# The gate of a Mamba block computed on GpSimd, behind its additions, instead of on VectorE

## The reference

```
x = x + 0.5 * ffn(layernorm(x))          # 8 experts, top 2, 128 -> 512 -> 128, silu
x = x + mixer(layernorm(x))
x = x + 0.5 * ffn(layernorm(x))

mixer(x):   out1 = mamba(rmsnorm(x));  x1 = x + out1
            out2 = memory(mamba(rmsnorm(x1)));  return x1 + out2

mamba(u):   xm, res = split(u @ in_w + in_b)          # 256 channels each
            xm = silu(causal_conv(xm));  delta, B, C = projections of xm
            h[t] = h[t-1] * exp(delta*A) + delta*xm*B     # 16 states for each channel
            y = sum over states of h*C
            y = (y + xm * D_ssm) * silu(res)              # the gate: what is moved
            return y @ out_w + out_b
```

## Time and profile before

| | |
|---|---|
| median of the runs | 2010.15 us (2008.85 to 2011.12) |
| profiled execution | span 2008.6 us, from its first to its last instruction; no other time of it is given |
| PE | 1699.4 us busy (85%) |
| DVE | 1722.4 us (86%) |
| ACT | 1144.8 us (57%) |
| POOL | 748.6 us (37%) |
| mean granted TensorE clock | 0.865 |
| DVE: scans L912 | 256 of 2523 ns |
| DVE: gate, L930, L933, L936 | 32 x 682, 64 x 481, 32 x 692 ns |
| POOL: additions L1101 | 192 of 2866 and 32 of 2846 ns |

### The profile page before, as it was taken

The page is one execution under the profiler, slowest core; times in us unless marked ns, Lnnn a source line. Parts: engine busy times, 40 slices in busy tenths (PEclk is TensorE's granted clock), DMA queues, the critical chain, the costliest instruction groups (busy, mean ns, idle before and its releaser), DMA issues. The chain is left out here.

```text
span 2008.6 us, 26762 instructions
## 1 busy us (share of the span) xinstructions
PE 1699.4 (85%) x8800; PEld 1325.2 (66%) x8800; DVE 1722.4 (86%) x2419; ACT 1144.8 (57%) x2206; POOL 748.6 (37%) x366
## 2 busy tenths in 40 slices
PE   5779667889989898989899898998989899659778
PEld 4657535767767677767677676776767677436667
DVE  4269998999989998998989899898989899999931
ACT  3266554655756665656666566655756558436622
POOL 0005353444424244444324344243434444443310
PEclk9889767988989798998998799897989789668869
DMA  5000000000000000000000000000000000000000
GB/s 157 1 6 1 1 0 1 6 0 1 2 12 1 1 1 7 6 1 1 1 12 2 1 1 7 6 1 1 1 6 1 0 1 1 5 1 1 1 6 6
DMA packets 11432, 13.40 MB, mean 7 GB/s; under 512 B 400, under 2 KB 8592, under 8 KB 11152
## 3 DMA queue, kind: packets, MB, share of 16 engines
q1 hardware_dynamic: 11280, 11.51, 1.9%
HBM read 9.41 MB, written 2.10 MB: 6 GB/s over the span
## 5 line engine op out<-in xcount | busy, mean ns | idle before, releaser
L1101 POOL TENSOR_TENSOR acc<-acc,G 128x1024 f32<-128x1024 f32 x192 | 550.3, 2866 | 500.8 <-DVE G L922 495.1
L912 DVE TENSOR_TENSOR_SCAN hs<-dA,dbu 128x1024 f32<-128x1024 f32 x256 | 641.3, 2523 | 3.0 <-ACT dA L625 2.1
L568 ACT ACTIVATE raw<-b_h 128x512 f32<-128x512 f32 x512 | 305.4, 599 | 437.0 <-PE b_h L328 423.4
L625 ACT ACTIVATE dA<-delta,A 128x255 f32<-128x255 f32 x1024 | 423.0, 495 | 32.0 <-DVE hs L912 16.0
L922 DVE TENSOR_TENSOR G<-hs,b_r 128x1024 f32<-128x1024 f32 x256 | 310.0, 1211 | 29.3 <-PE b_r L407 21.3
L407 PE MATMUL b_r<-bcr,selr 64*128 64x256 f32 x1024 | 247.0, 346 | 89.6 <-DVE G L922 37.8
L902 DVE TENSOR_TENSOR dbu<-du,b_r 128x1024 f32<-128x1024 f32 x256 | 308.2, 1209 | 9.8 <-PE b_r L407 9.2
L326 PE MATMUL b_h<-xh,w1h 128*128 128x512 f32 x512 | 253.9, 496 | 73.3 <-DVE xa L838 26.4
L407 PEld LDWEIGHTS b_r<-bcr,selr 64*128 64x128 f32 x1024 | 162.2, 207 | 195.3 <-issue 89.2
L335 PE MATMUL b_h<-w2s,raw 128*128 128x128 f32 x2048 | 273.0, 286 | 0.0
L335 PEld LDWEIGHTS b_h<-w2s,raw 128*128 128x128 f32 x2048 | 251.3, 198 | 14.3 <-issue 4.5
(11 more groups left out here) (143 smaller groups left out, 1718.2 us busy)
## 6 DMA issues: line engine op xcount, KB each, us to landing
xin<-x_dram SPq DMA_DIRECT2D x8, 256.0 KB, 2.8
raw<-w_dram SPq DMA_DIRECT2D x1, 2048.0 KB, 11.5
out_dram<-ob SPq DMA_DIRECT2D x8, 256.0 KB, 2.3
prm<-pack_dram SPq DMA_DIRECT2D x1, 1124.5 KB, 5.2
dA<-early_dram SPq DMA_DIRECT2D x1, 512.0 KB, 11.8
hs<-sel_dram SPq DMA_DIRECT2D x2, 256.0 KB, 13.2
G<-sel_dram SPq DMA_DIRECT2D x2, 256.0 KB, 7.7
dbu<-early_dram SPq DMA_DIRECT2D x1, 384.0 KB, 11.9
```

What stands on the lines that cost most here:

```text
L568: do(hT[e % 2][:, c, :], H[i % 2][:, :], ACT.Silu).then_inc(f_hact, 1)
L625: last = do(dA[j % 4][:, d, k, 1:], delta[b][:, k, 1:], ACT.Exp, scale=A[:, k, s:s + 1])
L912: V.tensor_tensor_scan(flat(hs[j % 2]), flat(dA[j % 4]), flat(dbu[j % 2]), 0.0, ALU.mult, ALU.add)\
L1101: Q.tensor_tensor(acc[b][:, :, :, :], (G[0] if j == 1 else acc[b])[:, :, :, :], G[j % NG][:, :, :, :], ALU.add).then_inc(q_gs, 1)
```

## The change

The gate leaves VectorE's four lists and stands first in GpSimd's four lists, right behind a7 of the slot before and ahead of a1. GpSimd has no use for the combined multiply-add there: it multiplies xm by D_ssm into the first half of acc (two instructions of 128x256), adds that to yg, and multiplies by sres. That is five instructions and three drains where there were four and two. The waits are the same. TensorE's `memory_2` has one wait more, for the xb of the sequence before, which VectorE's order had implied so far.

```diff
     "vector": (
-        "gate flow b0 flog ftop b1 s0 s1 ...
+        "flow b0 flog ftop b1 s0 s1 ...
-        "f3 fstats gate b0 b1 s0 xsum s1 un ...
+        "f3 fstats b0 b1 s0 xsum s1 un ...
-        "flow b0 flog gate s0 b1 g0 xsum ...
+        "flow b0 flog s0 b1 g0 xsum ...
-        "f2 b0 b1 f3 s0 gate g0 b2 s1 s2 ...
+        "f2 b0 b1 f3 s0 g0 b2 s1 s2 ...
     "gpsimd": (
-        "a1 a2 a3 a4 a5 a6 a7",
-        "rms rs froot a1 a2 a3 a4 a5 a6 a7",
-        "rms a1 a2 rs lnx rmsx a3 a4 a5 a6 a7",
-        "a1 a2 a3 a4 froot a5 a6 a7"),
+        "gate a1 a2 a3 a4 a5 a6 a7",
+        "gate rms rs froot a1 a2 a3 a4 a5 a6 a7",
+        "gate rms a1 a2 rs lnx rmsx a3 a4 a5 a6 a7",
+        "gate a1 a2 a3 a4 froot a5 a6 a7"),
...
             def memory_2(g, b):
                 pe.wait_ge(g_oT, 2 * g + b + 1)
+                wait(pe, g_xb, 2 * g + b)
...
-            def gate_y(g, i):
-                q, b = 4 * g + i, i % 2
-                dve.wait_ge(q_gs, (q + 1) * (NP - 1))
-                dve.wait_ge(q_res, 2 * q + 2)
-                wait(dve, q_omm, q)
-                V.tensor_tensor(yg[:, :, :], acc[b][:, 0, :, :], acc[b][:, 1, :, :], ALU.add)
-                dve.drain()
-                for k in range(HALVES):
-                    V.scalar_tensor_tensor(out=yg[:, k, :], in0=xm[b][:, k, :], scalar=par("D_ssm")[:, k:k + 1],
-                                           in1=yg[:, k, :], op0=ALU.mult, op1=ALU.add)
-                dve.drain()
-                V.tensor_tensor(yg[:, :, :], yg[:, :, :], sres[b][:, :, :], ALU.mult).then_inc(q_yg, 1)
...
+            def gate_y(g, i):
+
+                q, b = 4 * g + i, i % 2
+                pool.wait_ge(q_gs, (q + 1) * (NP - 1))
+                pool.wait_ge(q_res, 2 * q + 2)
+                wait(pool, q_omm, q)
+                Q.tensor_tensor(yg[:, :, :], acc[b][:, 0, :, :], acc[b][:, 1, :, :], ALU.add)
+                pool.drain()
+                for k in range(HALVES):
+                    Q.tensor_scalar(acc[b][:, 0, k, :], xm[b][:, k, :], par("D_ssm")[:, k:k + 1], 0.0,
+                                    ALU.mult, ALU.add)
+                pool.drain()
+                Q.tensor_tensor(yg[:, :, :], yg[:, :, :], acc[b][:, 0, :, :], ALU.add)
+                pool.drain()
+                Q.tensor_tensor(yg[:, :, :], yg[:, :, :], sres[b][:, :, :], ALU.mult).then_inc(q_yg, 1)
```

More of the change, by code:

```diff
@@ L988, in slot @@
                                 square_norm(nxt, 0, ln, range(TILES))
[L989 to L992, removed]
+                    elif name in ("xsum", "mask", "xb"):
+                        if tail:
                             {"xsum": first_sum, "mask": masked, "xb": mixer_sum}[name](tail[0], tail[1] % 2)
@@ L1033, in finish @@
             def finish():
-                gate_y(GROUPS - 1, 3)
                 masked(GROUPS - 1, 1)
@@ L1114, in slot @@
                         pair_sum(g, i, num)
+                    elif name == "gate":
+                        if tail:
+                            gate_y(*tail)
                     elif name == "rms":
@@ L1135, in finish @@
             def finish():
+                gate_y(GROUPS - 1, 3)
                 ffn_root(second(GROUPS - 1))
```

## The result

The changed kernel takes 2041.26 us (median of 4 runs, 2038.94 to 2043.05), the kernel before 2009.50 us on the same chip (4 runs, 2008.69 to 2011.12): ratio 1.0159, 95% interval 1.0144 to 1.0173. It is 1.6% slower, 31.8 us, where I forecast 16.8; 2041 lies above the range of the main forecast alone (2015 to 2038) and inside the wide one (1996 to 2044). The profiled execution has a span of 2039.1 us and a time of 2040.94; its granted clock is 0.861 in the mean, 0.865 before.

A forecast was written before the change was run, and what follows sets the result against it. VectorE looked like the bound (92.7% busy), but each slot entry was priced separately: 15.2 + 0 - 11.3 + 10.2 + 2.7 = +16.8 us on 2010.15 gives 2027 us; range 2015 to 2038 alone, 1996 to 2044 wide.

The forecast's parts named there:

- main forecast: Whole kernel: 16.8 us slower, 2027 us, by itself 2015 to 2038; chance 0.5.
- the wide one: Whole kernel: the range 1996 to 2044 us, allowing for part of the rivals.
- What the gate costs on GpSimd: Each gate: three additions, two products and three drains take 5.03 us on GpSimd, against 2.32 on VectorE.
- Slot 1, first term: Entry to slot 1: a scan precedes the gate's last step, x1 comes 1.9 us later, 8 times: +15.2 us.
- (c): Whole kernel: products at 0.62, three steps between the xn, slot 3 at -0.7: +32 us, 2042; chance 0.15.
- Slot 3, the step that failed: Entry to slot 3 and the last group's slot 0: scans done 1.25 us sooner, 9 times: -11.3 us.
- Slot 2: Entry to slot 2: yg arrives before TensorE needs it, x1 stays, VectorE waits 3.9 us: 0, 8 times.
- Slot 0: Entry to slot 0: gate steps get among the four xn, which end 1.7 us later, 6 times: +10.2 us.
- The end: After the last addition of all, nothing covers the gate, so its longer time counts: +2.7 us.
- (a): Whole kernel: VectorE time is what counts, so removing its gates gives 1941 us; chance 0.05.
- (b): Shared port: GpSimd's next step precedes a waiting scan, xn go through in one: -10 to -15, about 1997; chance 0.15.
- (d): All scans: shifts change which scans meet an addition and could cancel the sum, about 2012 us; chance 0.15.

The follow-up runs named there:

- e4: The kernel before with the gate's arithmetic on no engine, yg a constant but for four elements written right after the last addition: 1956.40 us.
- e10: The same program as e2 (gate back on VectorE where slot 1 is entered), run once more with a profile: 2012.92 us.
- e7: The kernel before with one edit of VectorE's slot 0 list, dbu 1 and scan 0 ahead of the wait for lg: 1983.56 us.
- e9: Gate left out and yg released early as in e4, with GpSimd running the gate's five instructions on data nobody reads: 1973.07 us.
- e3: The changed kernel with VectorE's first scan in slot 1 behind x1 instead of ahead of it: 2027.89 us.
- e8: The changed kernel with e3's edit, e7's edit and one more scan ahead of x1 in slot 2: 1997.83 us.
- e1: The kernel before with the gate moved to GpSimd only where slot 1 is entered, 8 of 32 gates: 2029.19 us.
- e11: Gate left out, but yg released late, behind five GpSimd operations of 128x4: 2012.15 us.
- e2: The changed kernel with the gate back on VectorE where slot 1 is entered: nine runs, 2011.90 to 2014.86 us (5) and 2028.54 to 2030.12 (4).
- e6: The kernel before, gate kept on VectorE, with GpSimd also running copies of the gate's five instructions into a dead acc: 2064.85 us.
- e5: The changed kernel with ScalarE in slot 3 doing its second FFN piece ahead of sres and xm: 2038.26 us.

## Why the prediction came out as it did

The sign and the place were right: slot 1's entry, by yg's lateness. The size was half.

**What the gate costs on GpSimd.** Forecast 5.03 us; measured, where nothing is in the way, 0.23 + 1.27 + 0.17 + 0.95 + 0.15 + 1.28 + 0.14 + 1.27 = 5.46. The additions were right (1.27). The products take 0.479 us each and not 0.40, and I had left out the gap of 0.23 behind the last addition. The rule on one-input operations that I weighed ("GPSIMD Engine Reference", section 4.1, of the Trainium skill), taken without a fixed part, would have made them 0.22; the measurement is over twice that. In slot 1, with the scan in between, yg comes 7.25 us behind the last addition (634.19 - 626.94), forecast 7.09.

**Slot 1, first term: right mechanism, too small.** The order is the one forecast: scan served ahead of the last step, TensorE standing 3.33 (forecast 3.3). x1 came 3.0 late each time instead of 1.9. Of the 1.1 difference 0.16 is the gate itself and 0.93 the projection, 3.00 us instead of 2.07: the granted clock in 634.2 to 637.3 is 0.68, and 0.50 right behind it. The prediction had taken 2.07 from before, where it runs at 1.00, and named the clock only in rival (c). In the rest of the slot, which I had counted at 0, 7.8 us come back, since VectorE arrives later at its waits for TensorE's spreads. These waits fall from 2.6 us to 1.5 in groups 1 to 5. Net the term is +16.7 against 15.2: that it comes so near is luck, since two things that I had left out nearly cancel.

**Slot 3, the step that failed.** I wrote "745.32 becomes 744.07: -1.25" and "ACT's waits for yg stand 1 to 3 us behind it in slot 3 [...]; 0". The scans do go sooner: 6.47 us behind the last addition (755.19 - 748.72) against 8.47 (745.32 - 736.85). The gate's last step then holds them for 1.0 (5.47 for the two instead of 4.47), so that behind them 1.0 us is won, near the forecast. But the sum stopped there and carried this gain on to the end of the slot, and the next thing that VectorE needs is bcr, which ScalarE writes. From the delta ahead of the slot to bcr it is 23.86 us before (753.27 - 729.41), 23.25 in e4, 23.36 in e10 and 24.45 in the changed kernel. So even with no gate at all this group wins 0.6 us, and not 1.25; the same goes for groups 1 to 6 of e10 (0.5 or less each). Only e4's groups 1, 3 and 5 win more (1.8), where VectorE waits 0.2 us for bcr. What sets bcr early or late there was not looked for.

The changed kernel loses instead, since yg is late for ScalarE too. It is there 7.6 us behind the last addition (the second product waits for a scan, 3.07 for the two): sres waits 0.99 (2.4 in groups 1, 3, 4 and 5), TensorE stands 2.08 for the activation behind it (3.4 to 3.5 there), six FFN matmuls at half clock follow (759.15: 0.63 us, 0.40 at full clock), and VectorE waits 1.56 for bcr. Against e10 that is 1.1 us for each of these five groups. In group 6 the clock stays and the stretch is 0.7 longer all the same; why stays open. In sum it is +1.4 us instead of -11.3: this one step is 12.7 of the 13.7 us by which sum and measurement differ, and the rest nearly cancels.

A table of this stand of TensorE in slot 3 of groups 1 to 6 shows which kernels have it, with the L327 and L380 behind it:

| kernel | TensorE stands, us | at half clock behind it |
|---|---|---|
| before, e4, e7, e9 | 0.97 to 0.99 (6) | none |
| e3, e8, e10 | 0.97 to 1.07 (5), 1.60 to 1.63 (1) | none |
| e1 | 0.98 (5), 2.22 (1) | the one behind 2.22 |
| e11 | 0.98 (1), 1.35 to 1.43 (4), 2.83 (1) | the one behind 2.83 |
| e2 (upper group) | 1.58 (1), 2.06 to 2.11 (5) | the five: 3.67 for L380, not 1.94 |
| e6 | 1.90 (1), 3.04 to 3.08 (5) | the five: 0.63 for L327, not 0.40 |
| after | 0.98 (1), 2.08 (1), 3.44 to 3.49 (4) | the five: 0.63 for L327 |

(e5 has another order there.)

So a gate on GpSimd alone doesn't bring it on (e3, e8 and e10 have one), and it comes with the gate on VectorE too (e1 and e6). It hangs on whether ScalarE is at sres before yg is there, and for how long. In e10 the spread of C starts 3.92 us behind the last addition (before: 3.98) and ScalarE is busy until 748.17, past yg's end at 747.68; in the changed kernel the spread starts 2.57 behind it and ScalarE is free early. Why one program falls into the one or the other from run to run stays open.

**Slot 2**: 0.00 in seven of eight groups, and x1's wait 3.81 (forecast 3.9). I had not looked at group 0, whose slot 2 has no FFN matmuls to hide yg: +2.88.

**Slot 0**: xn x4 takes 4.05, not the 4.8 forecast: +1.0 and not +1.7. One gate step gets in between the four, and the product doesn't. With what falls off behind it: +7.2 instead of 10.2.

**The end**: +3.3 for 2.7.

**What it is made of.** e4, e9 and e11 take the change apart: without any gate 1956.4; with GpSimd's operations and nobody waiting 1973.1; with yg late and no large operation 2012.2; with both, the changed kernel, 2041.3. So

- taking the gate from VectorE: 1956.4 - 2010.1 = -54 us;
- yg late: 2012.2 - 1956.4 = +56 us;
- GpSimd's operations in VectorE's way: 1973.1 - 1956.4 = +17 us;
- what the two cost together beyond their sum: 2041.3 - 1956.4 - 55.8 - 16.7 = +12 us.

The four medians were not all taken on one chip; beside them the kernel before has 2009.3 to 2010.1 us, so the last term is good to a few us only. By places, with the same subtraction made on the traces (13.4 us in sum), it lies in slot 3 (3.1), slot 0 (3.1), slot 2 (2.7), the last group's slot 0 (2.5) and ahead of the first x1 (1.9). In slot 1 it is 0.3: -2.4 up to x1 and +2.6 behind. It is thus not at slot 1's entry, where I had first looked for it, and which of the waits makes it is not shown.

**Rivals.** (a), VectorE time counts, has its share: 54 of 74 us were to be had, where the prediction had 11 and my expectation of e4 30. It lost because it priced only what goes away. (b) is refuted by the 3.06. (c) was the nearest: the sum is within 1 us of its +32, but that is luck in the main. Of its reasons only the clock in slot 1 came, not products at 0.62 or three steps between the xn, and it too had a gain in slot 3. (d) is out: a mean of 2600 ns for a scan, not 2523; no cancelling.

## What to carry to other kernels

An operation moved from a full engine to an idle one is priced by two numbers, the time that it frees there and the time by which its result comes later for those who wait; here 2.32 us freed, 32 times, were worth 54 us in all, and 3 to 5 us of lateness cost 56. A gain is only priced when the sum has gone on to the next thing that the engine waits for: in slot 3 that was bcr, and the forecast's 1.25 us were lost there. Where the loaded engine already has waits, look first for work to put into them: one reordered list (e7) brought 26 us, more than the move could bring in the best order found (e8, 12). And a short new wait of TensorE must be priced with the half clock that can follow it, in matmuls that stand some places further on.

## What the runs showed of the hardware

- The clock after a stand of TensorE: in slot 3 the granted clock stays 1.00 behind stands of 0.97 to 1.90 us, and falls to 0.50 behind stands of 2.06 to 3.49 (table above), for 3.4 us in the changed kernel (758.2 to 761.6) and 6.8 in e2 (756.4 to 763.2). The length of the stand doesn't settle it everywhere: in slot 1 of e3 the clock falls at 637.3, behind a stand of 1.52 that ends at 635.52. A program can sit on that edge: e2's nine runs split 5 to 4, 16 us apart, and the two traces differ by a stand of 0.98 or 2.1 us in slot 3 of five groups.
- A GpSimd operation of 128x4 doesn't hold a scan (2.28 us in e11, where it starts within one), yet is held by it: 5.69 us for four, 3.95 elsewhere. How few elements it takes to wait isn't shown.
- The Trainium skill ("SBUF — State Buffer", "SBUF: two separate sides") calls the shared port an exclusive lock. For large operations the rows agree (3.36 and 3.06 above); beside small ones they don't: in e11 the scan starts at 624.68 within one that lasts to 625.05, and still takes 2.28, so that GpSimd alone pays.
- VectorE's xn with one GpSimd addition among the four: 4.05 against 3.06 us, less than the addition's 1.27.
